# First cross attention, first batch: the mask is added to the scores by TensorE, and the maxima are taken by one plain maximum a slot

## The chip, the cores and the metric

The program runs on one core of one Trainium2 chip. The core has TensorE (PE, matrix products into PSUM), VectorE (DVE), ScalarE (ACT), GpSimd (POOL) and SyncE (SP, which issues most transfers here); each works through its own list of instructions, and semaphores tie the lists together. The time is that of one launch on the device, in microseconds; a kernel's time is the median of its runs.

## What is computed

The reference is a decoder of four layers over x (4 batches of 256 tokens, 128 features) with a context of 4 batches of 512 tokens. Only the cross attention of the first layer matters here. It has 16 heads of 8 features, a mask over queries and keys, and takes its keys and values from the context without a projection:

```python
v = value.reshape(N, Sv, HEADS, HEAD_DIM)
k = key.reshape(N, Sk, HEADS, HEAD_DIM)
q = query.reshape(N, Sq, HEADS, HEAD_DIM)
energy = jnp.einsum('nqhd,nkhd->nhqk', q, k)
energy = jnp.where(mask == 0, jnp.float32(-1e+20), energy)
attention = jax.nn.softmax(energy / jnp.sqrt(jnp.float32(E)), axis=3)
out = jnp.einsum('nhql,nlhd->nqhd', attention, v).reshape(N, Sq, E)
out = out @ W_fc.T + b_fc
```

## The kernel before

**Slots.** Each attention is a row of slots, written out by hand; TensorE, VectorE and ScalarE each have a function for a slot (`l0a_slot` for the first self attention, `cross_slot` for the cross attentions). The first cross attention, X0, has 64 slots for its scores, 16 for each batch: slot t treats a pair of heads (t // 2 % 8) and one of the two tiles of 128 queries (t % 2). Its first slots run together with the last ones of the self attention: X0's slot 0 is the 36th of `l0a_slot`.

**Scores and maxima.** `scores_of` computes the scores of one head for 128 queries and 512 keys into half of a PSUM tile of two banks, `ps_s`; the two heads of the pair (parity 0 and 1) lie at rows 0 and 64 of `q_stack` and `ctx_stack`, since their queries and keys are split into parts of bf16 and use 56 rows each (49 in the last two batches). There are two such tiles, taken in turn by `ring`; TensorE may write one again once VectorE has counted `maxed`. The maxima are taken by `greatest` on VectorE: for X0 two times `tensor_tensor_reduce`, each of which adds the mask `far_q` (0, or -2^66 where a key is masked; bf16, written by GpSimd, counted by `far_done`) to 512 scores of each row and keeps the row's maximum. The other cross attentions use one `tensor_reduce` over both banks, which also negates. After 16 slots `split_max` turns the negated maxima into three parts of bf16; for X0 it negates them first. `turn_max` turns them, VectorE copies them into `mT` (L1884), and SP writes them as rows into `q_stack` (`max_rows`, L2862).

**Exponentials.** They follow 20 slots behind (`LEAD`), from the keys' side: `exps_of` computes the scores again, transposed, with the maxima as extra rows, and adds the transposed mask `far_k` in the same way as is done for the scores below: a matmul of the identity with the mask starts the bank (L606), the scores are added to it (L608). ScalarE takes the exponential (L1396), and `sums` (L672) multiplies with the values. X0's slot 20 can't begin before the maxima's rows of the first batch have landed (`d_maxrow`).

**Around it.** In the same slots TensorE finishes the self attention: its exponentials' scores (L608), its sums (L672), the turning of its groups (L577, after ScalarE has lifted them, L1384), the closing (L585, L593, L554), the building of stacks (`stack_unit`, L698, copied by ScalarE, L1424) and the transposing of the mask (`turn_mask`, L764). The last closing gives the queries of the fourth batch, which GpSimd splits (L2635 to L2638) and SP writes and fills (L2809, L2821) ahead of the first rows of maxima: SP has one list, in this order:

```python
        for b in (2, 3):
            cross_inputs(X0, b)
        max_rows(X0, 0)
```

Of the kernel before, what the change touches and what calls it, by code (L numbers as in the profile page):

```python
# [32 lines left out]
B, S, S2, E = 4, 256, 512, 128  # L33
H, D = 16, 8
TPB = S // P
NT = B * TPB
# [71 lines left out]
A0, X0, A1, X1, X2 = "L0a", "L0x", "L1a", "L1x", "L2x"  # L108
# [16 lines left out]
def close_slot(use, b):  # L125
    return 21 + 8 * b if use == A0 else 40 + 16 * b


def order_of(pairs):
    return {p: i + 1 for i, p in enumerate(pairs)}  # L130
# [21 lines left out]
LAST = {A0: 54, X0: 96, X1: 96, X2: 93, "chain": 125}  # L152
CFILL = {X0: 32, X1: 128, X2: 192}
PLACED = 2
POOL_SQUARES = range(4, 8)
NORM_LATE = (3, 5)
SQUARES = order_of([(u, j) for u in range(8) for j in range(4) if u not in POOL_SQUARES or j >= 2])
Q_ROW = 24
# [3 lines left out]
def fills_before(use, b):  # L162
    return {A0: 0, X0: 1, A1: 0, X1: 1, X2: 2}[use] + (2 if b >= PLACED and use in (A1, X1, X2) else 0)

# [25 lines left out]
def stack_count(kind, b):  # L190
    return max(STACK_N[unit] for unit in stack_units(kind, b)) + 1
# [51 lines left out]
def build(nc, d, out, ctx):  # L243
    def sb(name, shape, dt=F32):
        return ctx.enter_context(nc.sbuf_tensor(name, shape, dt))

    def semaphore(name):
        return ctx.enter_context(nc.semaphore(name))

    pe, dve, act, pool, sp = nc.tensor, nc.vector, nc.scalar, nc.gpsimd, nc.sync  # L250
# [7 lines left out]
    ctx_stack = sb("ctx_stack", [P, PAIRS, CTX], BF16)  # L258
# [7 lines left out]
    ident_b = sb("ident_b", [P, P], BF16)  # L266
# [35 lines left out]
    def wk(lo, n):  # L302
        return work[:, lo:lo + n]
# [16 lines left out]
    def rows_by_head(tile):  # L320
# [22 lines left out]
                for part in (ffn_w[:, ROOM_AT + 3072:ROOM_AT + 5120], wk(4096, 2048))]  # L343
# [4 lines left out]
    far_q = wk(0, 2048).bitcast(BF16).rearrange("p (t k) -> p t k", t=NT)  # L348
# [11 lines left out]
    ps_s = [ctx.enter_context(nc.psum_tensor(f"ps_s{i}", [P, 2, 512], F32)) for i in range(2)]  # L360
# [36 lines left out]
    ctx_ps, ctx_done, gram_ps, gram_done, ctx_bias, c_split, kx_split, far_done, farT_ps, farT_done = (  # L397
        semaphore(n) for n in ("ctx_ps", "ctx_done", "gram_ps", "gram_done", "ctx_bias", "c_split", "kx_split",
                               "far_done", "farT_ps", "farT_done"))
# [56 lines left out]
    def rows_of(use, b):  # L456
        return (K_STACK, K_STACK, Q_ROW + 1) if use in (A0, X0) and b < PLACED else (K_SCORE, K_EXP, ROW_MAX)

# [77 lines left out]
    def tensor_program():  # L536
# [27 lines left out]
        def turn_max(use, b, tile):  # L564
            n = BATCH0[use] + b + 1
            i = tile()
            pe.wait_ge(max_split, n)
            pe.transpose(ps_s[i][0:96, 0, 0:64].bitcast(BF16), mparts[:].rearrange("p a s c -> p (a s c)"),
                         ident_b[:]).then_inc(max_ps, 1)
            free[f"s{i}"] = (max_T, n)  # L570

        def turn_group(use, g, tile):
            n = GROUP0[use] + g + 1
            i = tile()
            pe.wait_ge(lifted, n)
            for q in range(TPB):
                m = pe.transpose(ps_s[i][:, 0, q * P:(q + 1) * P], outT[:, g % 2, q * P:(q + 1) * P], ident)  # L577
            m.then_inc(turned, 1)
            free[f"s{i}"] = (weighed, n)
# [37 lines left out]
        def scores_of(use, h, parity, i):  # L617
            p0 = parity * SLOT
            b = h // PERIOD[use]
            n_rows = rows_of(use, b)[0]  # L620
            if use == A0:
                pair = h % 8
                for q in range(TPB):
                    m = pe.matmul(ps_s[i][:, parity, q * S:(q + 1) * S],  # L624
                                  q_stack[p0:p0 + n_rows, b, pair, q * P:(q + 1) * P],
                                  self_stack[p0:p0 + n_rows, b, pair, :], start=True, stop=True)
                return m
            pair, part = h // 2 % 8, h % 2
            return pe.matmul(ps_s[i][:, parity, :], q_stack[p0:p0 + n_rows, b, pair, part * P:(part + 1) * P],  # L629
                             ctx_stack[p0:p0 + n_rows, pair, b * S2:(b + 1) * S2], start=True, stop=True)  # L630

        def pair_step(use, t, tile):
            h = t - LEAD[use]
# [5 lines left out]
            if scores:  # L639
                i = tile()  # L640
                if t % PERIOD[use] == 0:
                    b = t // PERIOD[use]
                    if use == A0 and b < PLACED:
                        pe.wait_ge(stacked, max(stack_count("q", b), stack_count("k", b)))
                    elif use == X0 and b < PLACED:
                        pe.wait_ge(stacked, max(stack_count("x", b), stack_count("c", b)))
                    else:
                        pe.wait_ge(d_qfill[b], 32 * (fills_before(use, b) + 1))
                    if use == A0 and b >= PLACED:
                        pe.wait_ge(d_kfill[b], 32)  # L650
                        pe.wait_ge(d_ones, 160)
                    if use == X0 and b >= PLACED:
                        pe.wait_ge(d_cfill, CFILL[X0])
# [145 lines left out]
                    turn_norm("L0x", b)  # L799

        def cross_slot(use, t, w_out, following, tile=ring):
            if t == 0 and use != X0:
                pe.wait_ge(d_ones, 192)
                pe.wait_ge(d_cfill, CFILL[use])
            if t == LEAD[use] and use == X0:
                pe.wait_ge(farT_done, B)
            if t == LEAD[use] + 4:
                pe.wait_ge(d_vload, 16 * {X0: 1, X1: 2, X2: 3}[use])
            if t < STEPS[use] + LEAD[use]:
                pair_step(use, t, tile)  # L810
            if t % 16 == 1 and t > 1 and t < 80:
                turn_max(use, (t - 17) // 16, tile)
            g, k = divmod(t - LEAD[use] - 4, 4)
            if 0 <= g < 16:
                m = sums(use, g, k, 4 * g + 2 + k // 2, 4, cross_values)
                m.then_inc(summed, 1)
                free["v"] = (lifted, GROUP0[use] + g + 1)
            g, rest = divmod(t - LEAD[use] - 8, 4)
            if rest == 0 and 0 <= g < 16:
                turn_group(use, g, tile)  # L820
            for b in range(B):
                at = t - close_slot(use, b)
                if at == 2:
                    turn_close(use, b)
                if at == 3:
                    project_out(use, b, w_out, tile)
                if at == 6 and following:
                    turn_norm(following, b)
# [537 lines left out]
    def scalar_program():  # L1366
# [267 lines left out]
        def l1_sqrt(u):  # L1634
            act.wait_ge(least_sq, u + 1)
            act.activation(small[:, 1, 0:16], small[:, 0, 0:16], ACT.Sqrt, bias=minus1[:]).then_inc(rooted_s, 1)
            for n, g in enumerate(HALVES):
                if n == 0 and u in POOL_SQUARES:
                    act.wait_ge(l1_pool_sq, u - POOL_SQUARES[0] + 1)
                else:  # L1640
# [143 lines left out]
    def vector_program():  # L1784
# [63 lines left out]
        def greatest(use, t, tile):  # L1848
            i = tile()
            n = STEP0[use] + t + 1  # L1850
            dve.wait_ge(score_ps, n)
            if use == A0:
                b, pair = divmod(t, 8)
                m = dve.tensor_reduce(mx[:, b, :, pair, :], ps_s[i][:].rearrange("p a (q k) -> p a q k", q=TPB),  # L1854
                                      AX, ALU.max, negate=True)
            else:
                b, pair, part = t // 16, t // 2 % 8, t % 2
                if use == X0:
                    for parity in range(2):
                        m = dve.tensor_tensor_reduce(ps_s[i][:, parity, :], ps_s[i][:, parity, :],  # L1860
                                                     far_q[:, b * TPB + part, :], 1.0, -3e38, ALU.add, ALU.max,
                                                     mx[:, b, parity, pair, part:part + 1])
                else:
                    m = dve.tensor_reduce(mx[:, b, :, pair, part], ps_s[i][:], AX, ALU.max, negate=True)  # L1864
            m.then_inc(maxed, 1)
            if t % PERIOD[use] == PERIOD[use] - 1:
                split_max(use, b, n)

        def split_max(use, b, n):
            col = mx[:, b, :, :, :].rearrange("p a h q -> p a (h q)")  # L1870
            dve.wait_ge(maxed, n)
            if use == X0:
                settle(dve.tensor_scalar(col, col, -1.0, None, ALU.mult))
            settle(dve.tensor_copy(mparts[:, :, 0, :], col))
            settle(dve.tensor_tensor(col, col, mparts[:, :, 0, :], ALU.subtract))
            settle(dve.tensor_copy(mparts[:, :, 1, :], col))
            dve.tensor_tensor(mparts[:, :, 2, :], col, mparts[:, :, 1, :], ALU.subtract).then_inc(max_split, 1)
# [735 lines left out]
    def gpsimd_program():  # L2613
# [96 lines left out]
        def l1_attention():  # L2710
# [18 lines left out]
            for u in range(2 * B):  # L2729
# [7 lines left out]
                if u == 1:  # L2737
                    split_keys(A1, 3, map_T, 8)
                    split_queries(A1, 3, map_T, 7)
                if u + 2 in POOL_SQUARES:  # L2740
                    l1_squares(u + 2)
# [382 lines left out]
```

## Time and profile before

| | |
|---|---|
| median of 3 runs | 1243.61 us (1237.75 to 1248.25) |
| the profiled execution | 1246.88 us, span 1245.6 us |
| TensorE busy | 1028.6 us, 83% of the span |
| VectorE busy | 800.2 us, 64% |
| ScalarE busy | 612.5 us, 49% |
| GpSimd busy | 252.0 us, 20% |
| mean granted clock of TensorE | 0.867 |
| first and last masked maximum (L1860, 128 in all) | 117.6 and 261.3 us |

The rows further down come from the hardware profiler's record of one execution. Times are microseconds from the span's start. A chain of waits follows the work that ended last back to what released it. Durations of matmuls overlap, so that the distance between two starts says more than a duration; "x2" behind a row is two instructions merged. The granted clock is 1.00 for 2.4 GHz and 0.50 for 1.2 GHz.

### The profile page before, as it was taken

Reading aid. Unit: us, or ns where it says so; the run is one execution under the profiler, and the core shown is the slowest. Engines: PE = TensorE matmul, PEld = TensorE weight load, DVE = VectorE, ACT = ScalarE, POOL = GpSimd, SP = SyncE. Lnnn points to the kernel's source line nnn. Section 1 sums busy time; section 2 is a strip of 40 time slices with the busy share of each in tenths; the row PEclk is TensorE's granted clock in tenths of the full one; section 3 lists DMA queues with packets and bytes.
Section 4 is the critical chain, followed back from the end, with each engine's and each line's share of the span. In section 5 each row is a group of like instructions: output and inputs, shape, how many; then the busy total and the mean of one; then the engine's idle time right before and its main releaser. Section 6 shows DMA issues by size and latency. Waiting matters only on the chain.

```text
span 1245.6 us, 19903 instructions
## 1 busy us (share of the span) xinstructions
PE 1028.6 (83%) x7630; PEld 550.0 (44%) x7649; DVE 800.2 (64%) x2016; ACT 612.5 (49%) x1018; POOL 252.0 (20%) x309
## 2 busy tenths in 40 slices
PE   5777779999899974778867889999658868779999
PEld 4233313333667652345532333566412333437767
DVE  7786867751324467877777882677688887665412
ACT  2456436566433527678763777323115546433342
POOL 2833210000000225477551000001222001000000
PEclk9778869999999996566776997999858989879999
DMA  8323040000000210068013201700101200100000
GB/s 302 94 72 85 27 179 2 2 2 2 1 1 1 77 54 7 1 186 156 17 45 125 116 2 19 125 1 1 52 26 33 97 1 2 34 1 1 1 9 9
DMA packets 34785, 61.23 MB, mean 49 GB/s; under 512 B 4771, under 2 KB 25076, under 8 KB 33092
## 3 DMA queue, kind: packets, MB, share of 16 engines
q1 hardware_dynamic: 33828, 58.64, 16.7%
q8 instruction: 61, 1.00, 0.3%
q10 hardware_dynamic: 864, 1.33, 0.3%
q14 instruction: 32, 0.26, 0.1%
HBM read 42.91 MB, written 16.65 MB: 48 GB/s over the span
## 4 chain that ended last, share of the span: by engine, by line
PE 59%; DVE 27%; ACT 5%; issue 4%; POOL 3%; DMA 2%; SPq 1%; DVEq 0%; POOLq 0%; ACTq 0%
PE ps_s L879 10%; PE ps_e L869 9%; PE ps_v L672 6%; DVE mx L1864 6%; PE ps_e L608 5%; PE ps_s L629 3%; PE ps_e L606 3%; DVE ps_s L1860 2%; PE ps_e L973 2%; PE ps_s L960 2%; ACT work L1396 2%; DVE mx L1854 2%; DVE stats L1802 1%; DVE xn L1820 1%; PE ps_v L1144 1%
## 5 line engine op out<-in xcount | busy, mean ns | idle before, releaser
L1396 ACT ACTIVATE work<-ps_e 128x512 f32<-128x512 f32 x448 | 250.7, 598 | 148.1 <-PE ps_e L608 142.8
L2622 POOL TENSOR_TENSOR rstd<-rstd,halves 128x2 f32<-128x2 f32 x52 | 36.6, 704 | 699.0 <-DVE rstd L1807 698.8
L1864 DVE TENSOR_REDUCE mx<-ps_s 128x2 f32<-128x1024 f32 x128 | 154.1, 1222 | 27.8 <-PE ps_s L629 26.3
L629 PE MATMUL ps_s<-ctx_stack,q_stack 49*128 49x512 bf16 (+1 forms) x384 | 128.5, 453 | 47.1 <-DVE mx L1864 34.8
L608 PE MATMUL ps_e<-q_stack,ctx_stack 52*128 52x256 bf16 (+1 forms) x768 | 149.7, 297 | 16.8 <-issue 6.3
L1498 ACT ACTIVATE work<-ps_s,keep 128x512 f32<-128x512 f32 x136 | 93.1, 687 | 140.4 <-PE ps_s L879 137.5
L672 PE MATMUL ps_v<-work,vaug 128*32 128x256 f32 x1536 | 132.0, 420 | 4.8 <-ACT work L1384 4.8
L869 PEld LDWEIGHTS ps_e<-ffn_w,work 128*128 128x128 f32 x960 | 117.9, 196 | 21.0 <-issue 19.9
L879 PE MATMUL ps_s<-xnT,ffn_w 128*128 128x512 f32 x240 | 119.4, 623 | 3.6 <-ACT work L1498 3.6
L869 PE MATMUL ps_e<-ffn_w,work 128*128 128x128 f32 x960 | 119.7, 280 | 0.8 <-DVE x L2054 0.8
L2064 DVE SCALAR_TENSOR_TENSOR x<-ps_e,gates,x 128x128 f32<-128x128 f32 x128 | 38.9, 346 | 121.7 <-PE ps_e L869 118.7
L1860 DVE CUSTOM_DVE_ANT_0 ps_s<-ps_s,work 128x512 f32<-128x512 f32 x128 | 86.0, 717 | 30.4 <-PE ps_s L629 30.3
L608 PEld LDWEIGHTS ps_e<-q_stack,ctx_stack 52*128 52x128 bf16 (+1 forms) x768 | 44.6, 97 | 105.3 <-ACT work L1396 49.1
L629 PEld LDWEIGHTS ps_s<-ctx_stack,q_stack 49*128 49x128 bf16 (+1 forms) x384 | 29.3, 97 | 75.0 <-DVE mx L1864 48.8
L879 PEld LDWEIGHTS ps_s<-xnT,ffn_w 128*128 128x128 f32 x240 | 42.4, 198 | 42.6 <-issue 25.9
L672 PEld LDWEIGHTS ps_v<-work,vaug 128*32 128x32 f32 x1536 | 31.7, 112 | 49.8 <-issue 37.3
L2681 POOL TENSOR_TENSOR work<-work 128x1536 f32<-128x1536 f32 x14 | 48.0, 3448 | 0.2
L1854 DVE TENSOR_REDUCE mx<-ps_s 128x4 f32<-128x1024 f32 x32 | 38.2, 1220 | 11.1 <-PE ps_s L624 10.7
L606 PE MATMUL ps_e<-work,ident_b 128*128 128x512 bf16 x109 | 44.4, 408 | 0.0
L1376 ACT ACTIVATE xnT<-ps_m 128x256 f32<-128x256 f32 x36 | 13.7, 382 | 61.1 <-PE ps_m L554 59.8
L1895 DVE RECIPROCAL rsum<-ps_s 128x8 f32<-128x8 f32 x48 | 9.8, 203 | 49.9 <-PE ps_s L577 49.7
L577 PE MATMUL ps_s<-keep,work 128*128 128x128 f32 x128 | 29.9, 318 | 13.2 <-ACT work L1384 6.5
(380 smaller groups left out, 1815.7 us busy)
## 6 DMA issues: line engine op xcount, KB each, us to landing
q_stack<-q_scr SPq DMA_DIRECT2D x32, 192.0 KB
ffn_w<-in_L0f_w SPq DMA_DIRECT2D x1, 4608.0 KB, 14.7
ffn_w<-in_L1f_w SPq DMA_DIRECT2D x1, 3456.0 KB, 13.1
q_scr<-parts SPq DMA_DIRECT2D x16, 192.0 KB, 2.1
c_scr<-ffn_w SPq DMA_DIRECT2D x12, 256.0 KB, 7.7
kx_scr<-ffn_w SPq DMA_DIRECT2D x12, 256.0 KB, 4.2
ctx_stack<-kx_scr SPq DMA_DIRECT2D x2, 1536.0 KB
ctx_stack<-c_scr SPq DMA_DIRECT2D x2, 1536.0 KB
```

Source lines behind the costliest of these rows:

```text
L606: pe.matmul(bank[name], ident_b[:], far_k[:, b, k:k + 2, :].rearrange("p k q -> p (k q)"), start=True, stop=False, skip_group_check=True)
L608: m = pe.matmul(bank[name][:, half * S:(half + 1) * S], stack[p0:p0 + n_rows, pair, k * P:(k + 1) * P], q_stack[p0:p0 + n_rows, b, pair, : ...
L629: return pe.matmul(ps_s[i][:, parity, :], q_stack[p0:p0 + n_rows, b, pair, part * P:(part + 1) * P], ctx_stack[p0:p0 + n_rows, pair, b * S ...
L672: m = pe.matmul(ps_v[j * COLS:(j + 1) * COLS, 0:S], values(b * nkt + k, g % 4 * GROUP + j), pt[:, j % 2, k % 2, :], start=(k == 0), stop=( ...
L869: m = pe.matmul(bank[name][:, i * P:(i + 1) * P], hid[:, j, (t0 + i) * P:(t0 + i + 1) * P], w2(e, j), start=(j == 0), stop=(j == FJ - 1))
L879: pe.matmul(bank[name], w1_of(st, e, j), xnT[:, g * 512:(g + 1) * 512], start=True, stop=True).then_inc(UPS[st], 1)
L1396: act.activation(pt[:, parity, :, :].rearrange("p k q -> p (k q)"), bank[f"e{parity}"], ACT.Exp).then_inc(exped, 1)
L1498: act.activation(hid_unit(st, u)[:, j, :], bank[f"h{n % 2}"], ACT.Gelu_apprx_tanh, bias=b1).then_inc(HIDS[st], 1)
L1854: m = dve.tensor_reduce(mx[:, b, :, pair, :], ps_s[i][:].rearrange("p a (q k) -> p a q k", q=TPB), AX, ALU.max, negate=True)
L1860: m = dve.tensor_tensor_reduce(ps_s[i][:, parity, :], ps_s[i][:, parity, :], far_q[:, b * TPB + part, :], 1.0, -3e38, ALU.add, ALU.max, mx ...
L1864: m = dve.tensor_reduce(mx[:, b, :, pair, part], ps_s[i][:], AX, ALU.max, negate=True)
L2681: pool.tensor_tensor(c, c, l1_s[:, HALVES[n], :], ALU.add).then_inc(added, 1)
```

## The change

For the first batch of X0 (`MASK_ON_PE = 1`: batches under 1), `scores_of` starts each bank with a matmul of the identity and `far_q` over 128 rows and 512 columns, and the scores are added to it. `greatest` then takes the plain, negated maximum over both banks, as for the other cross attentions, and `split_max` leaves its negation out. TensorE waits for all of `far_q` at slot 0. The other three batches are as they were.

```diff
@@ -152,6 +152,7 @@
 LAST = {A0: 54, X0: 96, X1: 96, X2: 93, "chain": 125}
 CFILL = {X0: 32, X1: 128, X2: 192}
 PLACED = 2
+MASK_ON_PE = 1
 POOL_SQUARES = range(4, 8)
 NORM_LATE = (3, 5)
 SQUARES = order_of([(u, j) for u in range(8) for j in range(4) if u not in POOL_SQUARES or j >= 2])
@@ -626,8 +627,11 @@
                                   self_stack[p0:p0 + n_rows, b, pair, :], start=True, stop=True)
                 return m
             pair, part = h // 2 % 8, h % 2
+            masked = use == X0 and b < MASK_ON_PE
+            if masked:
+                pe.matmul(ps_s[i][:, parity, :], ident_b[:], far_q[:, b * TPB + part, :], start=True, stop=False)
             return pe.matmul(ps_s[i][:, parity, :], q_stack[p0:p0 + n_rows, b, pair, part * P:(part + 1) * P],
-                             ctx_stack[p0:p0 + n_rows, pair, b * S2:(b + 1) * S2], start=True, stop=True)
+                             ctx_stack[p0:p0 + n_rows, pair, b * S2:(b + 1) * S2], start=not masked, stop=True)
 
         def pair_step(use, t, tile):
             h = t - LEAD[use]
@@ -799,6 +803,8 @@
                     turn_norm("L0x", b)
 
         def cross_slot(use, t, w_out, following, tile=ring):
+            if t == 0 and use == X0:
+                pe.wait_ge(far_done, NT)
             if t == 0 and use != X0:
                 pe.wait_ge(d_ones, 192)
                 pe.wait_ge(d_cfill, CFILL[use])
@@ -1855,7 +1861,7 @@
                                       AX, ALU.max, negate=True)
             else:
                 b, pair, part = t // 16, t // 2 % 8, t % 2
-                if use == X0:
+                if use == X0 and b >= MASK_ON_PE:
                     for parity in range(2):
                         m = dve.tensor_tensor_reduce(ps_s[i][:, parity, :], ps_s[i][:, parity, :],
                                                      far_q[:, b * TPB + part, :], 1.0, -3e38, ALU.add, ALU.max,
@@ -1869,7 +1875,7 @@
         def split_max(use, b, n):
             col = mx[:, b, :, :, :].rearrange("p a h q -> p a (h q)")
             dve.wait_ge(maxed, n)
-            if use == X0:
+            if use == X0 and b >= MASK_ON_PE:
                 settle(dve.tensor_scalar(col, col, -1.0, None, ALU.mult))
             settle(dve.tensor_copy(mparts[:, :, 0, :], col))
             settle(dve.tensor_tensor(col, col, mparts[:, :, 0, :], ALU.subtract))
```

TensorE's list in X0's slots 0 and 1, before (ps_s are the scores' tiles, L629; L577 turns a group of the self attention, L764 transposes the mask):

```order
L554 MATMUL ps_m<-keep,xn 128x128 x2
L629 MATMUL ps_s<-ctx_stack,q_stack 128x512 x2
L608 MATMUL ps_e<-q_stack,self_stack 128x256 x4
L577 MATMUL ps_s<-keep,work 128x128 x2
L629 MATMUL ps_s<-ctx_stack,q_stack 128x512 x2
L764 MATMUL ps_m<-ident_b,work 128x128 x8
```

and after, where the lines are some further down (L632 is the mask, L633 the scores):

```order
L555 MATMUL ps_m<-keep,xn 128x128 x2
L632 MATMUL ps_s<-work,ident_b 128x512
L633 MATMUL ps_s<-ctx_stack,q_stack 128x512
L632 MATMUL ps_s<-work,ident_b 128x512
L633 MATMUL ps_s<-ctx_stack,q_stack 128x512
L609 MATMUL ps_e<-q_stack,self_stack 128x256 x4
L578 MATMUL ps_s<-keep,work 128x128 x2
L632 MATMUL ps_s<-work,ident_b 128x512
L633 MATMUL ps_s<-ctx_stack,q_stack 128x512
L632 MATMUL ps_s<-work,ident_b 128x512
L633 MATMUL ps_s<-ctx_stack,q_stack 128x512
L768 MATMUL ps_m<-ident_b,work 128x128 x8
```

Where two matmuls of 56 rows stood side by side, four now alternate between 128 rows and 56.

VectorE's list from slot 0 to the first maximum of slot 1, before (L1860 is the masked maximum and the read of its result; L1911 to L1929 are the self attention's):

```order
L1860 ISA ps_s,mx<-ps_s,work 128x512
L1860 ISA mx 128x1
L1860 ISA ps_s,mx<-ps_s,work 128x512
L1860 ISA mx 128x1
L1911 RECIPROCAL rsum<-ps_s 128x8
L1913 TENSOR_SCALAR rsum<-rsum,lam 128x4
L1915 TENSOR_TENSOR work<-ps_s,rsum 128x128
L1921 TENSOR_TENSOR xn<-work 128x32 x2
L1927 TENSOR_TENSOR work<-xn 128x256
L1928 TENSOR_REDUCE l0a_ss<-work 128x16
L1929 TENSOR_SCALAR l0a_ss<-l0a_ss 128x16
L1860 ISA ps_s,mx<-ps_s,work 128x512
```

and after:

```order
L1870 TENSOR_REDUCE mx<-ps_s 128x2
L1917 RECIPROCAL rsum<-ps_s 128x8
L1919 TENSOR_SCALAR rsum<-rsum,lam 128x4
L1921 TENSOR_TENSOR work<-ps_s,rsum 128x128
L1927 TENSOR_TENSOR xn<-work 128x32 x2
L1933 TENSOR_TENSOR work<-xn 128x256
L1934 TENSOR_REDUCE l0a_ss<-work 128x16
L1935 TENSOR_SCALAR l0a_ss<-l0a_ss 128x16
L1870 TENSOR_REDUCE mx<-ps_s 128x2 x2
```

Four instructions of a slot have become one; nothing else changed its place.

## Rows read from the trace of the kernel before

**Rows 1.** The page: the span, and busy time by engine
```profile
span 1245.6 us, 19903 instructions
```

**Rows 2.** Waits of PE, 112 to 166 us: us in total, times, longest
```profile
PE ps_s L629 <- DVE mx L1860: 6.3, 7, 1.6
```

**Rows 3.** Chain of waits, 112 to 185 us: start, length, what
```profile
117.57 0.70 DVE ps_s L1860
...
119.03 0.39 PE ps_s L629 x2
...
121.30 0.32 PE ps_s L629 x2
...
123.66 0.42 PE ps_s L577 x2
...
128.47 0.71 PE ps_s L593 x4
...
129.18 0.33 PE ps_s L629 x2
...
140.48 0.42 PE ps_s L577 x2
...
144.06 2.91 POOL l0a_ss L2622
...
147.78 0.66 PE ps_m L585 x2
...
165.92 0.39 PE ps_e L608
```

**Rows 4.** Timeline of PE: start, us, line, operation, tiles, shapes, count
```profile
117.02 0.39 PE L629 MATMUL ps_s<-ctx_stack,q_stack 56*128 56x512 bf16 x2
...
117.24 0.38 PE L608 MATMUL ps_e<-q_stack,self_stack 52*128 52x256 bf16 x4
...
126.58 0.39 PE L629 MATMUL ps_s<-ctx_stack,q_stack 56*128 56x512 bf16 x2
...
137.97 0.39 PE L629 MATMUL ps_s<-ctx_stack,q_stack 56*128 56x512 bf16 x2
...
153.68 0.66 PE L554 MATMUL ps_m<-keep,xn 128*128 128x128 f32 x2
```

**Rows 5.** Timeline, mask matmuls in the exponentials' bank, at either clock
```profile
166.46 0.61 PE L606 MATMUL ps_e<-work,ident_b 128*128 128x512 bf16 x1
...
167.00 0.61 PE L629 MATMUL ps_s<-ctx_stack,q_stack 56*128 56x512 bf16 x1
...
187.99 0.39 PE L629 MATMUL ps_s<-ctx_stack,q_stack 56*128 56x512 bf16 x1
...
188.31 0.39 PE L606 MATMUL ps_e<-work,ident_b 128*128 128x512 bf16 x1
...
188.63 0.39 PE L629 MATMUL ps_s<-ctx_stack,q_stack 56*128 56x512 bf16 x1
```

**Rows 6.** Timeline of DVE, end of a masked maximum; page, group of plain maxima
```profile
118.83 0.14 DVE L1860 DVE_READ_ACCUMULATOR2_ANT mx<- 128x1 f32 x1
...
L1864 DVE TENSOR_REDUCE mx<-ps_s 128x2 f32<-128x1024 f32 x128 | 154.1, 1222 | 27.8 <-PE ps_s L629 26.3
```

**Rows 7.** Windows: us, busy by engine (count), granted clock, DMA share, GB/s
```profile
147.80:156.00 8.20, 5.30 (x18) 1.97 (x18) 8.02 (x28) 0.77 (x2) 2.63 (x5) 0.50 0.14 48
...
165.90:178.50 12.60, 12.42 (x51) 2.74 (x52) 7.04 (x20) 6.09 (x11) 0.00 (x0) 0.50 0.77 329
...
178.50:185.00 6.50, 6.33 (x59) 1.97 (x59) 4.55 (x13) 4.72 (x9) 0.00 (x0) 1.00 0.00 0
```

**Rows 8.** Timeline of DVE, POOL and SP's queue before the wait at 165.9
```profile
160.55 0.21 DVE L1884 COPY mT<-ps_s 96x128 bf16<-96x128 bf16 x1
...
156.50 0.70 POOL L2638 TENSOR_TENSOR parts<-qT,parts 128x256 bf16<-128x256 f32 x1
...
161.39 1.56 SPq L2862 DMA_DIRECT2D q_stack<-mT  x2
```

## The prediction

> **What bounds the kernel now.** I read the page first for the span (1245.6 us [rows 1]), then the chain of waits and the waits of the stretch in which the changed slots run, 117 to 156 us, and last the timelines. I number the sixteen changed slots 0 to 15 (the first slots of the first cross attention, one pair of score matmuls L629 and one pair of masked maxima L1860 each). The chain [rows 3] shows the reader that this stretch isn't bound by one engine. It goes from TensorE to VectorE at 117.57, back to TensorE at 119.03, through TensorE's own row of work to 123.66, through VectorE to 128.47, again through TensorE (with short visits to ScalarE) to 140.48, then through VectorE and a 2.91 us power on GpSimd to 147.78, and ends in TensorE's start at 165.92, when the row of maxima for the exponentials has landed. So a us added to TensorE in slots 0 to 2 and 5 to 8 is a us on the path, and a us taken from VectorE counts in few places. TensorE does wait for the masked maxima, 6.3 us in 7 waits [rows 2], but three of these belong to the second batch, and twelve of the sixteen slots don't begin with such a wait.
>
> **What the change adds on TensorE.** Today the two score matmuls of a slot use 56 rows each, in different halves of the array; they start together, and the next instruction starts 0.22 us after them (117.02 to 117.24 [rows 4]) or, where it is one over all 128 rows, 0.32 us (129.18 plus 0.33 [rows 3]). The change puts a 128-row matmul of 512 columns ahead of each, so that mask, scores, mask, scores must go one after the other. The trace has exactly this succession, since the exponentials' bank gets its mask in the same way: scores at 187.99, mask at 188.31, next scores at 188.63 [rows 5]. That is 0.32 us a step at full clock (2.4 GHz, granted 1.00). At the lower level (1.2 GHz, 0.50) it is 0.54 (166.46 to 167.00 [rows 5]). A slot therefore holds TensorE for 4 x 0.32 = 1.29 us instead of 0.32: **0.97 us more**, and 4 x 0.54 - 0.54 = 1.62 us more at the lower clock. The masks alone, at 0.32 each, would be only 0.64; the other third is the lost overlap of the two score matmuls. VectorE's start moves from 0.55 us after the slot's first matmul (117.02 [rows 4] to 117.57 [rows 3]) to 0.97 + 0.55 = 1.52 us.
>
> The Trainium skill (TensorEngine Tiling, Key Properties) says that a change of the tiling mode drains TensorE; the step of 0.32 against 0.22 agrees with that. Its TensorE: Matmul & The Clock Gate, Back-to-back issue gap, would have 216 ns for 512 columns at full clock with no such drain; what that makes of the sum is a rival below.
>
> **What it takes from VectorE.** Before, a slot's bank pair is free 1.46 us after its maxima begin (117.57 to 119.03 [rows 3]: two custom operations, a read of the accumulator of 0.14 that ends at 118.97 [rows 6], 0.06 to the matmul). One plain maximum over 1024 elements takes 1.22 us (L1864 [rows 6]), with the same 0.06 it is 1.28: 0.18 less. Sixteen of these are 2.9 us, and one small negation (L1873) goes with its wait for the step before; at most about 0.3 us. This 3.2 us is the whole possible gain. The wait on the mask (far_done) costs nothing: the masks were already in use by VectorE at 117.57, behind the same count. The extra reads and weights have no DMA.
>
> **The sum, along the chain.**
> - Slot 0 to slot 1: + 0.97 - 0.18 = + 0.8 (slot 1 starts at 119.8, not 119.03).
> - Slots 1 and 2 lie in one row of TensorE work with the mask transposes L764 and the sums L672, and ScalarE's copy, lift and TensorE's L577 at 123.66 follow it: + 0.97 each, + 2.7 (L577 at 126.4).
> - Slots 3 and 4: today VectorE carries the path here and TensorE has about 0.4 us to spare (slot 4's pair at 126.58 [rows 4] is ready before VectorE is free, at 127.0). TensorE's work is now longer: slot 3 brings slot 4's start to + 3.7 (130.3), VectorE starts at 130.3 + 1.52 = 131.8, and frees the bank 1.28 later at 133.1, against 128.47: + 4.6.
> - Slots 5, 6, 7, 8: the first starts at 129.18 [rows 3], the last at 137.97 [rows 4], on TensorE's row of work to 140.48, four times 0.97: + 8.5 (L577 at 149.0).
> - 140.48 to 147.78: VectorE and GpSimd carry + 8.5 on. TensorE meanwhile has slots 9, 10, 11 with stack units and one mask transpose; 1.29 for each slot and the rest as long as before brings it to 156.6, a little later than the 156.3 of the other way: + 8.8.
> - 147.78 to L554 at 153.68 [rows 4], slots 12 to 15: today at the lower clock [rows 7]. With TensorE busy without a gap from 149.0 to 156.6 I take the full clock. L585 and slot 12 hold TensorE to 158.3; slot 12's maximum starts at 158.5 and ends at 159.7; the addition to x and its statistics are 1.35, as before; slot 13's maximum starts at 161.3, and slot 15 starts when that has freed its bank, 162.6, and ends at 163.9, where L554 follows: + 10.2.
> - Then the same work as before, without a mask matmul: ScalarE's copy, GpSimd's split whose last part starts at 156.50, SP's writes and fills, the row of maxima issued at 161.39 [rows 8], TensorE's start at 165.92 [rows 3]. VectorE's copy of the maxima, 160.55 [rows 8], ends 0.6 us before SP gets to them. It moves by about + 9 and stays hidden.
>
> So TensorE's start moves from 165.92 to 176.1: **+ 10.2 us**. Behind it TensorE runs 12.6 us at the lower clock before that rises [rows 7]; I take that unchanged, as TensorE is mostly idle for some us ahead of the start in both. Nothing later is changed, and almost all later transfers are issued behind work of this chain, so the delay is carried to the end. The profiled execution (span 1245.6, time 1246.88) would be 1257; it lay 3.3 above the median, so the median becomes 1243.6 + 10.2 = **1254 us**.
>
> **Rivals.**
> - *A mask step costs a plain stream* (0.12). With 0.22 us a step, the shortest step in the rows [rows 4], a slot takes 0.88, + 0.55; the same walk gives + 0.4, + 1.5, + 2.5, + 4.7 and about + 5 at the end: 1249. For it: a stream of 512 columns without a change of rows has that step. Against it: both changes, to 128 rows and back, are at 0.32 in [rows 5]. The page's 216 ns is the same case.
> - *VectorE was the bound, and the masks hide in TensorE's waits* (0.07). Then 3.2 us are won: 1240.5. For it: VectorE is busy 8.02 of 8.20 us from 147.8 to 156 [rows 7], and the 6.3 us of waits [rows 2]. It decides only if a slot's added TensorE time is under the 0.18 that VectorE gives back or lies in a wait in every slot; slots 5 to 8 speak against it.
> - *The clock falls in the last changed slots* (0.10). Today it is at the lower level from 147.8 on. If it fell at 156.6 as well, slots 12 to 15 would be four steps of 0.54 each, TensorE alone would carry slots 13 to 15, and L554 would start at 167.4 and not at 163.9: + 13.7, 1257. Against it: TensorE is now nearly always busy there.
> - *The clock stays up, or rises earlier, behind 176* (0.08). Ten pieces of 1.08 us would be 0.64 us each: 4.4 us back, + 6, 1249.5. Against it: TensorE idles some 7 us from 169 on.
> - That the change doesn't do what it says is out: the added instructions stand in the order of the rows above.
>
> **How the numbers follow.** The forecast has 0.60, and 0.03 is for anything else. Its own spread is about 3 us (a neighbour slot's wait misjudged, the clock's step after the start falling earlier or later, the three runs of before spreading over 10 us). The range reaches down to the two cases near 1249 with that spread, 1246, and up to the clock's case, 1262; it leaves out the gain. Over 1% is what a measurement of this kernel can tell from no change, 12.4 us here, so 1256 divides: of the forecast's 0.60 a quarter lies above, 0.15, and nearly the whole 0.10 of the fallen clock, with 0.02 of the rest: slower 0.27. Faster needs 1231, beyond even the rival that gains: 0.02. The rest, 0.71, is within 1%.
>
> **What would show it.** In the profile after: the succession mask, scores, mask, scores at 0.32 us a step; slot 1 near 119.8; L577 of 123.66 near 126.4; L593 of 128.47 near 133.1; L577 of 140.48 near 149.0; L554 near 163.9; exponentials starting near 176; a granted clock of 1.00 between 150 and 163. Wrong would be: steps of 0.22, a clock that falls earlier, or a stretch behind 176 that gives several us back.

## The result

The changed kernel takes **1251.69 us** (median of 20 runs, 1243.06 to 1262.86) against 1243.98 us for the one before (20 runs, 1236.35 to 1254.59): ratio **1.0065, 95% interval 1.0047 to 1.0083**, 8.1 us slower by that ratio (5.8 to 10.3; the medians are 7.7 us apart). The forecast was 10.2 us slower, 1254.

The first lines of the profile page of the changed kernel (for [rows 1]; busy us by engine, share and count of instructions behind it):

```profile
span 1252.0 us, 19913 instructions
...
PE 1039.5 (83%) x7656; PEld 554.6 (44%) x7681; DVE 796.6 (64%) x1967; ACT 612.5 (49%) x1018; POOL 252.4 (20%) x309
```

In its profiled execution slot 0 began 3 us earlier than in that of before, for reasons that lie ahead of the change, so the two stretches are compared from a mark of their own: the turning matmul L554 (L555 in the changed kernel, whose lines are some further down) right ahead of slot 0. Before, it stood here, in the timeline of TensorE:

```profile
116.64 0.44 PE L554 MATMUL ps_m<-keep,xn 128*128 128x128 f32 x2
```

The changed kernel's timeline of TensorE, from that mark over slot 0, slot 4, the end of slot 5, the last L555 behind slot 15 and the first scores for the exponentials (for [rows 4]; L632 is a mask, L633 scores, L578 and L586 are L577 and L585 of before; the record of slot 0's first mask is missing):

```profile
113.47 0.44 PE L555 MATMUL ps_m<-keep,xn 128*128 128x128 f32 x2
114.06 0.39 PE L633 MATMUL ps_s<-ctx_stack,q_stack 56*128 56x512 bf16 x1
114.38 0.39 PE L632 MATMUL ps_s<-work,ident_b 128*128 128x512 bf16 x1
114.70 0.39 PE L633 MATMUL ps_s<-ctx_stack,q_stack 56*128 56x512 bf16 x1
...
115.23 0.44 PE L578 MATMUL ps_s<-keep,work 128*128 128x128 f32 x2
...
126.41 0.44 PE L586 MATMUL ps_m<-keep,xn 128*128 128x128 f32 x2
126.69 0.38 PE L632 MATMUL ps_s<-work,ident_b 128*128 128x512 bf16 x1
...
131.33 0.84 PE L702 MATMUL ps_m<-parts,ffn_w 128*32 128x256 bf16 x24
...
159.39 0.44 PE L555 MATMUL ps_m<-keep,xn 128*128 128x128 f32 x2
...
171.33 0.39 PE L609 MATMUL ps_e<-q_stack,ctx_stack 56*128 56x256 bf16 x1 [4.86 <-issue]
```

Scores, mask, scores stand at 114.06, 114.38, 114.70: 0.32 us a step, as foreseen. From L554 to L577 it was 0.92 us before and is 1.76 now.

The chain of waits of the changed kernel (for [rows 3]; start, length, what):

```profile
116.47 0.39 PE ps_s L632
...
128.06 1.24 DVE mx L1870
...
129.34 0.71 PE ps_s L594 x4
...
145.04 0.41 PE ps_s L578 x2
```

and the waits of TensorE from 108 to 171 us (for [rows 2]):

```profile
PE ps_s L632 <- DVE mx L1870: 1.5, 2, 0.8
...
PE ps_s L633 <- DVE mx L1870: 0.7, 1, 0.7
PE ps_s L594 <- DVE mx L1870: 0.7, 1, 0.7
```

The slots' first matmuls had waited 6.3 us for maxima, those of the second batch included. Now it is 2.2 us for the plain maxima and 1.0 more for a masked one of the second batch. Measured from the mark, in us:

| mark | before | after | difference | forecast |
|---|---|---|---|---|
| L593 (L594), which waits for slot 4's maximum | 11.83 | 15.87 | + 4.0 | + 4.6 |
| L577 (L578) behind slot 8 | 23.84 | 31.57 | + 7.7 | + 8.5 |
| L554 (L555) behind slot 15 | 37.04 | 45.92 | + 8.9 | + 10.2 |
| first scores for the exponentials | 49.28 | 57.86 | **+ 8.6** | + 10.2 |

The windows of the changed kernel (for [rows 7]: stretch, its length, busy time by engine, granted clock, share of DMA, GB/s) show the clock, which stayed at 1.00 through the masked slots:

```profile
117.00:147.00 30.00, 24.84 (x281) 11.17 (x287) 17.70 (x44) 14.18 (x27) 6.02 (x8) 1.00 0.00 1
147.00:156.00 9.00, 8.07 (x71) 3.19 (x64) 7.24 (x13) 4.45 (x8) 3.51 (x2) 1.00 0.32 90
156.00:165.00 9.00, 4.95 (x18) 1.49 (x17) 8.69 (x21) 0.38 (x1) 5.92 (x11) 0.78 0.15 43
```

Before, it had been at 0.50 from 147.8 on. SP's queue issued the rows of maxima here (for [rows 8]):

```profile
166.89 1.54 SPq L2868 DMA_DIRECT2D q_stack<-mT  x2
```

It follows the copy of the maxima (165.24 plus 0.21 in this trace) by 1.4 us; before it was 0.6. So the copy was hidden here too.

### The profile page after: what moved, and what is told of

The parts are those of the page before. It is cut to its first block, busy times and chain, and to the rows that moved or that the text cites. A ratio compares the mean times of both kernels' runs of the same rounds, so it can differ in the third digit from the quotient of the medians.

```text
span 1252.0 us, 19913 instructions
## 1 busy us (share of the span) xinstructions
PE 1039.5 (83%) x7656; PEld 554.6 (44%) x7681; DVE 796.6 (64%) x1967; ACT 612.5 (49%) x1018; POOL 252.4 (20%) x309
## 3 DMA queue, kind: packets, MB, share of 16 engines
q8 instruction: 62, 1.02, 0.3%
## 4 chain that ended last, share of the span: by engine, by line
PE 61%; DVE 27%; ACT 5%; issue 4%; DMA 1%; POOL 1%; SPq 0%; DVEq 0%; ACTq 0%; POOLq 0%
PE ps_s L885 10%; PE ps_e L875 9%; PE ps_v L676 6%; DVE mx L1870 6%; PE ps_e L609 5%; PE ps_s L633 3%; PE ps_e L607 3%; PE ps_e L979 2%; DVE mx L1860 2%; ACT work L1402 2%; PE ps_s L966 2%; DVE ps_s L1866 2%; PE ps_s L1130 1%; DVE work L2349 1%; DVE xn L1826 1%
## 5 line engine op out<-in xcount | busy, mean ns | idle before, releaser
L1870 DVE TENSOR_REDUCE mx<-ps_s 128x2 f32<-128x1024 f32 x144 | 173.4, 1222 | 38.3 <-PE ps_s L633 36.6
L633 PE MATMUL ps_s<-ctx_stack,q_stack 49*128 49x512 bf16 (+1 forms) x384 | 134.2, 447 | 43.5 <-DVE mx L1870 35.3
L609 PE MATMUL ps_e<-q_stack,ctx_stack 52*128 52x256 bf16 (+1 forms) x768 | 149.9, 297 | 17.3 <-issue 7.1
L875 PE MATMUL ps_e<-ffn_w,work 128*128 128x128 f32 x960 | 118.7, 278 | 0.8 <-DVE x L2060 0.8
L609 PEld LDWEIGHTS ps_e<-q_stack,ctx_stack 52*128 52x128 bf16 (+1 forms) x768 | 44.7, 97 | 105.2 <-ACT work L1402 48.4
L1866 DVE CUSTOM_DVE_ANT_0 ps_s<-ps_s,work 128x512 f32<-128x512 f32 x96 | 64.6, 716 | 29.5 <-PE ps_s L633 29.5
L633 PEld LDWEIGHTS ps_s<-ctx_stack,q_stack 49*128 49x128 bf16 (+1 forms) x384 | 30.8, 97 | 72.9 <-DVE mx L1870 49.3
L607 PE MATMUL ps_e<-work,ident_b 128*128 128x512 bf16 x109 | 44.5, 408 | 0.0
L1860 DVE TENSOR_REDUCE mx<-ps_s 128x4 f32<-128x1024 f32 x32 | 38.1, 1218 | 9.9 <-PE ps_s L625 9.5
L578 PE MATMUL ps_s<-keep,work 128*128 128x128 f32 x128 | 29.7, 317 | 13.3 <-ACT work L1390 6.5
```

The lines of the kernel that those rows point to most:

```text
L607: pe.matmul(bank[name], ident_b[:], far_k[:, b, k:k + 2, :].rearrange("p k q -> p (k q)"), start=True, stop=False, skip_group_check=True)
L609: m = pe.matmul(bank[name][:, half * S:(half + 1) * S], stack[p0:p0 + n_rows, pair, k * P:(k + 1) * P], q_stack[p0:p0 + n_rows, b, pair, : ...
L875: m = pe.matmul(bank[name][:, i * P:(i + 1) * P], hid[:, j, (t0 + i) * P:(t0 + i + 1) * P], w2(e, j), start=(j == 0), stop=(j == FJ - 1))
```

## Experiments

**The order of masks and scores; TensorE's part alone; VectorE's part alone.** Four kernels on one chip, each against the same runs of the kernel before (27, median 1244.19 us).

The first puts both masks of a slot ahead of its scores:

```diff
-            if masked:
-                pe.matmul(ps_s[i][:, parity, :], ident_b[:], far_q[:, b * TPB + part, :], start=True, stop=False)
+            if masked and parity == 1:
+                for k in range(2):
+                    pe.matmul(ps_s[i][:, k, :], ident_b[:], far_q[:, b * TPB + part, :], start=True, stop=False)
```

> The changed kernel, with both masks of a slot ahead of both score matmuls (mask, mask, scores, scores). The theory (the cost is the order: masks over 128 rows between scores of 56 rows cost the scores their overlap and a switch each): the second mask starts 0.22 us after the first, the scores 0.32 us after that, together; a slot holds TensorE some 0.86 us in place of 1.29, and the exponentials of the first batch start 4 to 5 us after those of before, counted from slot 0, not 8.7: ratio to before 1.003 to 1.005. The rival (any 128-row matmul costs 0.32, whatever stands beside it, and the scores don't overlap behind a mask): no difference from the changed kernel, 1.0065.

Measured: 1247.80 us, ratio 1.0049 (1.0026 to 1.0072). Its timeline of TensorE, at the mark, at slot 1 (L633 masks, L634 scores) and at the first scores for the exponentials:

```profile
115.12 0.44 PE L555 MATMUL ps_m<-keep,xn 128*128 128x128 f32 x2
...
117.70 0.60 PE L633 MATMUL ps_s<-work,ident_b 128*128 128x512 bf16 x2 [0.80 <-DVE mx L1871]
118.24 0.39 PE L634 MATMUL ps_s<-ctx_stack,q_stack 56*128 56x512 bf16 x2
118.56 0.62 PE L769 MATMUL ps_m<-ident_b,work 128*128 128x128 bf16 x8
...
167.83 0.39 PE L609 MATMUL ps_e<-q_stack,ctx_stack 56*128 56x256 bf16 x1
```

Two masks take 0.54 us and the two scores together 0.32: 0.86 us a slot, as expected. From the mark to the exponentials it is 52.7 us: + 3.4 against before, not + 8.6. So the order alone, with the same work, is worth 5.2 us; the rival, by which any 128-row matmul costs 0.32, falls. By the times the two orders can't be told apart surely (their intervals overlap); the traces tell them apart.

The second keeps the masked maxima:

```diff
-                if use == X0 and b >= MASK_ON_PE:
+                if use == X0:
-            if use == X0 and b >= MASK_ON_PE:
+            if use == X0:
```

> The changed kernel with the masked maxima of before: TensorE's masks are added, VectorE's work is that of before (a masked key gets the mask twice, which changes no result). Theory (TensorE's masks are the whole cost, VectorE gives back little, as it carries the path in few slots): the exponentials of the first batch start 9.5 to 10.5 us later than before, counted from slot 0; ratio 1.007 to 1.009. Rival (VectorE's 0.18 us a slot come back in every slot): 11.5 us and 1.009 to 1.010.

Measured: 1253.39 us, ratio 1.0095 (1.0060 to 1.0130).

```profile
114.69 0.44 PE L555 MATMUL ps_m<-keep,xn 128*128 128x128 f32 x2
...
119.60 1.04 PE L768 MATMUL ps_m<-ident_b,work 128*128 128x128 bf16 x8
...
162.80 0.44 PE L555 MATMUL ps_m<-keep,xn 128*128 128x128 f32 x2
...
174.81 0.39 PE L609 MATMUL ps_e<-q_stack,ctx_stack 56*128 56x256 bf16 x1 [4.89 <-issue]
```

From the mark to the exponentials it is 60.1 us, + 10.8, between the two expectations (9.5 to 10.5, and 11.5). But this execution can't be set beside the others as it stands: its granted clock was 0.50 from 118.7 to 122 us, in slots 1 and 2. The eight transposes L768 of slot 1 take 1.04 us there, 0.62 in the changed kernel's profile, and from slot 1's first mask to L578 behind slot 2 it is 8.0 us (117.92 to 125.94) against 6.55 (116.47 to 123.02), with no wait for VectorE in either. So 1.5 of the 10.8 are the clock. Without them it would be about + 9.4 (an estimate from these rows), just under the theory's side: with the masks on TensorE, VectorE's faster maxima give back some 0.8 us of the 3.2 that were reckoned as their most, and not the 10.8 - 8.6 = 2.3 that the two totals suggest. The masks aren't shown to have caused the fall: the profile of before has such a dip too, ahead of slot 0 (0.73 on the mean of 108 to 112 us).

The third leaves the mask out of the first batch's maxima altogether:

```diff
-            masked = use == X0 and b < MASK_ON_PE
+            masked = False
```

> The kernel before with one plain maximum a slot in the first batch and no mask matmul: the mask is left out of that batch's maxima (it still is in the exponentials). Theory: VectorE carries the path in slots 0, 3 to 4 and 12 to 15 only, so 1 to 1.5 us come of the 3.2 us that VectorE saves; ratio 0.999 to 1.000. Rival (VectorE bounds the batch): 3 us, 0.9975.

Measured: 1243.61 us, ratio 0.9983 (0.9958 to 1.0009), no difference by the times.

```profile
115.48 0.44 PE L555 MATMUL ps_m<-keep,xn 128*128 128x128 f32 x2
...
151.55 0.66 PE L555 MATMUL ps_m<-keep,xn 128*128 128x128 f32 x2
...
163.69 0.39 PE L609 MATMUL ps_e<-q_stack,ctx_stack 56*128 56x256 bf16 x1 [4.86 <-issue]
```

From the mark it is 48.2 us, - 1.1. VectorE's part alone was worth 1.1 us at most, as the theory had it. It is - 0.4 up to L578 behind slot 8 (138.96), and the rest comes in slots 12 to 15, where this profile still had the clock at 1.00 up to some 150 us (L586 at 146.26 took 0.41 us, where L585 took 0.66 before), so part of it can be the clock.

The fourth is the changed kernel once more:

> The changed kernel itself beside the other three, for one chip's comparison. All theories: 1.0065 within its interval; from slot 0's first matmul to the exponentials 57.6 us, within 0.5 us of the first profile, if the path there is fixed by the program and only the clock's changes move it.

Measured: 1254.84 us, ratio 1.0079 (1.0049 to 1.0109); 57.9 us from the mark (115.94 to 173.83), 0.03 from the first profile. So within the stretch the same program gives the same time, as long as the clock stays up (in the second kernel's profile it didn't). Behind it this profile differs from the first. The scores for the exponentials begin at 173.83, and those at 178.11 already have the duration of the full clock:

```profile
173.83 0.39 PE L609 MATMUL ps_e<-q_stack,ctx_stack 56*128 56x256 bf16 x1 [4.90 <-issue]
...
178.11 0.28 PE L609 MATMUL ps_e<-q_stack,ctx_stack 56*128 56x256 bf16 x1
```

The clock rose some 4 us behind the start of the exponentials here, 13.6 us behind it in the first profile of the same kernel and 12.6 in that of before. The totals scatter too: from the first scores for the exponentials to the end of the span it was 1079.7 us before, 1080.7 after, and 1075.6, 1074.8, 1083.1 and 1073.7 in these four. The clock isn't all of that, since the first of the four had it at 0.50 for nearly 13 us and still took 1075.6.

**The price of one more mask.** Each mask matmul is issued twice:

```diff
-                pe.matmul(ps_s[i][:, parity, :], ident_b[:], far_q[:, b * TPB + part, :], start=True, stop=False)
+                for k in range(2):
+                    pe.matmul(ps_s[i][:, parity, :], ident_b[:], far_q[:, b * TPB + part, :], start=k == 0, stop=False)
```

> The changed kernel with each mask matmul issued twice (the sum then holds the mask twice, which changes no result). Theory: the second mask matmul costs 0.22 us, as it needs no change of the rows, 0.43 us a slot; the two orders of the masks differed by 0.43 us a slot too and by 5.15 us at the exponentials, so these start 5 us later again, 63 us from the matmul ahead of slot 0. Rival (a mask step is 0.32 whatever stands ahead of it): 0.64 us a slot, 65.5 us.

Measured: 1256.34 us in one run. The timeline of TensorE:

```profile
115.17 0.44 PE L555 MATMUL ps_m<-keep,xn 128*128 128x128 f32 x2
...
118.61 0.60 PE L633 MATMUL ps_s<-work,ident_b 128*128 128x512 bf16 x2 [0.80 <-DVE mx L1871]
119.14 0.39 PE L634 MATMUL ps_s<-ctx_stack,q_stack 56*128 56x512 bf16 x1
119.46 0.61 PE L633 MATMUL ps_s<-work,ident_b 128*128 128x512 bf16 x2
...
179.75 0.39 PE L609 MATMUL ps_e<-q_stack,ctx_stack 56*128 56x256 bf16 x1
```

Mask, mask, scores is 0.53 us (118.61 to 119.14), scores to the next mask 0.32. So a mask behind a mask costs 0.21 to 0.22 us, and a step with a change between 128 and 56 rows costs 0.1 more. From the mark to the exponentials it is 64.6 us, 6.7 more than the changed kernel: between the expectations again, but not for the rival's reason. Against the changed kernel, L594 moved by 2.2 us (18.0 from the mark; five slots of 0.43) and L578 behind slot 8 by 3.9 (35.5 from the mark; nine slots of 0.43); the 6.7 are sixteen slots of 0.42. The theory had carried over from the two orders that twelve slots count. With this much on TensorE all sixteen do.

**Masks on TensorE in more batches.** `MASK_ON_PE = 4`:

> The changed kernel with the masks on TensorE in all four batches. Theory (a slot of scores costs TensorE some 0.6 to 1 us more wherever it stands, and more so beside the exponentials, where the score matmuls of 56 rows ran together with others of 56 rows): 48 more slots, 25 to 45 us, ratio 1.025 to 1.042. Rival (in the later batches TensorE's waits for VectorE take the masks up): under 8 us, 1.013 at most.

Measured: 1409.86 us, the median of 1336.60, 1402.33, 1417.39 and 1417.50, some 13% over the 1245.44 us of before on that chip (the fastest 7%), where 2.5 to 4.2% were expected. The mean granted clocks of the four were 0.840, 0.792, 0.777 and 0.778: the three lower ones go with the three longer times. The profile is that of the run with 1402.33. From the start of the exponentials on, in one window, and its last part by itself:

```profile
166.00:466.00 300.00, 289.66 (x1117) 70.50 (x1136) 74.94 (x136) 85.86 (x151) 2.89 (x4) 0.50 0.05 18
...
400.00:466.00 66.00, 63.24 (x296) 17.28 (x299) 7.86 (x39) 25.57 (x45) 0.69 (x1) 0.50 0.00 1
```

and the kernel before, beside its own scores, and at the end of them and in the exponentials behind:

```profile
200.00:250.00 50.00, 46.90 (x394) 15.85 (x398) 37.09 (x119) 31.03 (x56) 0.72 (x1) 1.00 0.01 2
250.00:300.00 50.00, 48.23 (x381) 17.50 (x384) 18.85 (x79) 32.54 (x60) 1.40 (x2) 1.00 0.01 2
```

TensorE was busy for 290 of 300 us and its clock stayed at 0.50. The masked slots are only part of that: their last mask starts at 390.05. For the 76 us behind it TensorE had no masks of scores, only the rest of the exponentials, which the kernel before ran at 1.00 (its last maximum is at 261.3), and the clock did not come up. (The next expectation has the clock down until the masked slots were over; it was down for these 76 us more.) Its timeline of TensorE, beside the exponentials (L607 and L632 masks, L609 and L633 scores):

```profile
202.49 0.61 PE L632 MATMUL ps_s<-work,ident_b 128*128 128x512 bf16 x1
203.03 0.61 PE L633 MATMUL ps_s<-ctx_stack,q_stack 56*128 56x512 bf16 x1
...
203.57 0.61 PE L607 MATMUL ps_e<-work,ident_b 128*128 128x512 bf16 x1
204.12 0.39 PE L609 MATMUL ps_e<-q_stack,ctx_stack 56*128 56x256 bf16 x1
204.44 0.61 PE L632 MATMUL ps_s<-work,ident_b 128*128 128x512 bf16 x1
204.98 0.61 PE L633 MATMUL ps_s<-ctx_stack,q_stack 56*128 56x512 bf16 x1
```

Every step is a change of rows, 0.54 us at this clock for 512 columns and 0.32 for 256, and a slot took 4.9 us (maxima at 220.83, 225.73) where it takes about 2.1 at full clock in the kernel before. If the clock had stayed up, 48 slots of 0.6 to 1 us would have been 30 to 48 us, by the estimate behind the expectation (25 to 45); the rest came with the clock.

Whether that was the chip's chance or this kernel's doing, two more kernels were to tell. `MASK_ON_PE = 2`:

> The changed kernel with the masks on TensorE in the first two batches. In the run with all four, TensorE's clock stayed at its lower level from the start of the exponentials until the masked slots were over, 300 us. Theory (while score slots with masks run beside the exponentials, TensorE's row of single 128-row and 56-row steps doesn't bring the clock up, though it is busy): the clock rises some us after slot 31; slots 20 to 31 take 4.9 us each at the lower clock in place of about 2.1, some 30 us more than the changed kernel: ratio 1.025 to 1.035. Rival (the clock was down in that run by the chip's chance, nothing of this kernel): the clock rises some 13 us after the exponentials begin, and a slot costs 0.6 to 1 us more at full clock, 10 to 12 us: ratio 1.014 to 1.017.

Measured: 1284.24 us, ratio 1.0306 (1.0255 to 1.0358).

```profile
180.00:230.00 50.00, 48.58 (x171) 10.60 (x173) 14.66 (x17) 13.66 (x24) 0.00 (x0) 0.50 0.07 31
231.00:240.00 9.00, 8.25 (x74) 2.77 (x68) 6.21 (x20) 5.36 (x10) 0.00 (x0) 1.00 0.02 5
```

The last mask starts at 226.4 and the last maximum of a slot with masks at 227.56 in this trace, and the clock is up from 231 us, with the scores of the third batch beside the exponentials: the theory's side, in time and in place. `MASK_ON_PE = 4` with both masks of a slot first (the edit of the first experiment):

> All four batches with masks on TensorE, both masks of a slot ahead of its scores, as in the first experiment. Theory (what holds the clock down is the row of single steps with a change between 128 and 56 rows each; the longer the rows of full work, the sooner it rises): fewer changes a slot, the clock rises during the second batch and the kernel takes 1275 to 1300 us, ratio 1.025 to 1.045. Rival (any masks beside the exponentials hold it down): as with alternating masks, 1330 to 1420 us.

Measured: 1280.07 us, ratio 1.0251 (1.0191 to 1.0311). The slowest of its four runs, 1283.39 us, is 53 us under the fastest with alternating masks and the same matmuls (1336.60; the medians are 130 us apart), and its mean granted clocks were 0.864 to 0.875.

```profile
171.00:187.00 16.00, 15.67 (x53) 3.10 (x51) 6.13 (x5) 5.37 (x9) 0.00 (x0) 0.50 0.44 189
188.00:250.00 62.00, 60.24 (x424) 19.17 (x431) 32.46 (x46) 30.34 (x54) 0.72 (x1) 1.00 0.01 1
```

The clock rose while the masked slots went on, to 291.7 us. This run and the one with two batches were on one chip. So masks beside the exponentials don't hold the clock down as such; it stayed down where they alternate with the scores. Three things limit that. The alternation doesn't bring a clock down that is up: slots 0 to 15 ran at 1.00 with it, but for dips of some 3 us in the profiles of the second kernel and of that with two batches. It isn't the only row that fails to bring it up, as the 76 us behind 390 show. And the order also saves time at the lower clock: a slot took 3.45 us there (maxima at 174.87 and 178.32), not 4.9. What TensorE's clock reacts to these runs don't tell.

**No mask in the maxima at all.** The third kernel with all four batches:

```diff
-MASK_ON_PE = 1
+MASK_ON_PE = 4
-            masked = use == X0 and b < MASK_ON_PE
+            masked = False
```

> The kernel before with one plain maximum a slot in all four batches and no mask matmul: the mask is left out of the maxima altogether, and stays in the exponentials, whose shift then is an upper bound of the true maximum. The theory: the first batch gives 1.07 us as in the run before; in the other three VectorE's 0.18 us a slot count where TensorE waits for it, in about every second slot, some 4 us: ratio 0.995 to 0.997. Rival (TensorE carries the later batches too): 1 us, 0.999.

Measured: 1239.72 us, ratio **0.9963 (0.9938 to 0.9988)**. It beats both kernels, by some 5 us the one before and some 12 the changed one (measured on another chip), and the interval is on the theory's side, if narrowly (the rival had 0.999). A softmax may be shifted by any bound of its maximum; the mask is in the exponentials' own scores in any case. It holds as long as no masked score lies so far above the unmasked ones that their exponentials vanish, which the kernels that mask their maxima don't need. Where the gain comes from is shown only in part. The first batch gave nothing in this profile: the exponentials begin 50.2 us from the mark (116.34 to 166.50), 0.9 later than before, as a write of SP ahead of the maxima's rows (L2815) took 2.98 us and not 1.42. From there to the start of the last slot's maximum it is 91.5 us (to 258.04), 3.3 less than before (165.92 to 260.72); the theory had some 4. A part of the 3.3 can be the clock, which was at 0.50 for a shorter time here.

One more form, each mask as two halves of 64 rows so that the rows need no change at all, was not tried.

## Why the prediction was right, and where it was off

- **What bounds the stretch** was right. The chain runs through TensorE in most slots, TensorE's added time went onto it, and VectorE's part alone was worth 1.1 us at most.
- **0.97 us a slot** was right for the steps (0.32) but too much for the entry. A score pair behind a 128-row matmul had paid the change of rows itself (0.38 us from L554 to slot 0's pair before, 116.64 to 117.02); a mask doesn't (0.28 from L586 at 126.41 to slot 4's mask at 126.69). Slots 0, 3, 4, 7 and 8 come behind such a pair of 128-row matmuls, so five times 0.1 of the 8.5 us up to L577 weren't there. From L554 to L577 slot 0 cost 0.84, not 0.97. Slot 5, behind the four matmuls L593, didn't save it: from L593 to the next instruction behind the slot it was 0.97 us before (128.47 to 129.44) and is 1.99 now (129.34 to 131.33), 1.02 more. Most of the rest of the way to the 7.7 measured is VectorE's start, which I had at 1.52 us after a slot's first mask: in slot 4 it was 1.37 (126.69 to 128.06). The cost of a slot at its two ends is the main term that was mis-sized.
- **Slots 12 to 15**: + 1.4 was foreseen from L585 to L554, and + 1.0 measured (5.90 us before, 6.88 after). Of the difference 0.25 lie in slot 12, whose maximum began 1.65 us behind L586 (152.51 to 154.16) and not 1.9. The stay of the clock at 1.00 was right, and not by luck: it was at 1.00 in these slots in all eight profiles that have masks on TensorE, and fell at their start or within them in all three that have none.
- **Behind L554** I carried the delay on unchanged. It shrank by 0.3: L554 itself ran at full clock (0.44 us, 0.66 before), and so the split and SP's part began sooner.
- **Behind the start of the exponentials** I took 12.6 us at the lower clock as unchanged. It was 13.6 in the first profile (windows of the changed kernel, below) and some 4 in the second of the same kernel, so this term isn't fixed by the program, and that the first profile came near 12.6 is luck:

```profile
171.30:184.90 13.60, 13.10 (x58) 3.03 (x63) 7.07 (x21) 6.58 (x12) 0.00 (x0) 0.50 0.70 304
184.90:190.00 5.10, 5.10 (x45) 1.49 (x41) 4.14 (x12) 3.48 (x7) 0.00 (x0) 1.00 0.01 3
```

- **The rivals.** A plain stream's step of 0.22 fell: the rows show 0.32 at every change and 0.22 only between two masks. VectorE as the bound fell with the third kernel. The clock did not fall in slots 12 to 15. It did not stay up behind them, but in the second profile of the changed kernel it rose about 9 us earlier than in the first: this rival, which had 0.08, came in one of the two profiled executions, and how often it came in the 20 runs isn't known. What no rival priced is the lower clock beside the exponentials: alternating masks there went with a clock that stayed down, as the run with all four batches shows.
- **The sum** of the trace, + 8.6, and the ratio of the times, 8.1 (5.8 to 10.3), agree; 10.2 is inside the interval of the times and outside what the traces allow.

## What to carry to other kernels

Price a matmul by the step between it and its neighbours in a row of the same kernel, not by its own columns: two matmuls on different rows of the array run for the price of one, and a full-height matmul between them costs its own time, their overlap, and 0.1 us for each change. If such a matmul has to be added, put the ones of full height together (here the same work in another order gave back 5.2 of 8.6 us). And before moving an operation to another engine, ask whether it is needed: the maxima did not need the mask.

## What the runs showed of the hardware

TensorE's clock can stay at 1.2 GHz for 300 us while the engine is busy 97% of the time. For 224 of these us its work was a row of single matmuls that alternate between 128 and 56 (later 49) rows, and for 76 more the plain exponentials, which the kernel before ran at 2.4 GHz. The same matmuls with the two masks side by side had it at 2.4 GHz some 19 us after the exponentials began (168.4 to about 187.5). In one kernel, from one execution to the next, the rise came 13.6 or some 4 us after that start. A change between 128-row and 56-row matmuls of 512 columns made the step 0.32 us in place of 0.22 at full clock. The Trainium skill (TensorEngine Tiling, Key Properties) has a change of the tiling mode drain the engine, which agrees.
